# Half filter convolution: branch bodies of 48 products in place of 80, and one branch for each added stage in place of one for three

## The chip, the cores and the metric

The kernel runs on one core of a Trainium2 chip. The metric is the time of one execution on the device in microseconds (us), the median of the runs. Five engines work side by side: TensorE (PE in the profile; PEld is its weight load), VectorE (DVE), ScalarE (ACT), GpSimd (POOL) and SyncE (SP), which starts the loads.

## The reference, cut to what matters

The model is a convolution block, a mixture of experts, attention, and the mixture again. The change lies in the convolution:

```
n_blocks, block_size, ks = (128, 64, 16)
n_block_row = n_channels // block_size          # n_channels = 256 here: 4
cols = randint(k3, (n_blocks,), 0, n_block_row)
rows = randint(k4, (n_blocks,), 0, n_block_row)
...
o = conv1d(x_unfold, W, padding=[(ks - 1, 0)], feature_group_count=n_blocks)
y = zeros(batch, n_block_row, bs, t).at[:, rows].add(o)
```

Each of 128 blocks of 64 by 64 by 16 weights filters one group of 64 input channels (`cols`) and is added to one group of 64 output channels (`rows`). The input has 512 channels, so 8 groups exist, but the drawn `cols` and `rows` are 0 to 3. The kernel must be right for 0 to 7 too.

## The kernel before

The weights of all blocks with the same pair of input and output group are summed first, and the convolution is then done with the sums. The 16 taps are handled as 8 stages `st` of two taps each.

Stages 0 to 4 (`NPE = 5`): TensorE sums. A stage has 8 banks; `sum_bank(st, q)` (line 647) waits for 512 KB of weights and multiplies them, in 8 products of 64 columns (16 matmuls on the chip), by a one-hot matrix. `raw` is a ring of 6 loads, so the bank numbered c+6 is loaded when bank c is summed. ScalarE rounds each bank (`round_banks`), VectorE takes the low part (`low_banks`, line 505), and `sum_bank` of bank c waits for the low part of bank c-3.

Stages 5 to 7 (`ND = 3`, the added stages): VectorE adds each of the 128 blocks into `acc` (`add_block`, line 524, the groups named `cv_acc` at line 532), and these additions are spread between the `low_banks` of stages 1 to 4: 14 blocks ahead of stage 2, then 4, 5 and some 5 for each bank. Their weights come in 16 loads of 768 KB from GpSimd's queue (`tap_blocks`), in a ring of three.

`products` (line 657, matmuls at line 669) is the convolution proper: three matmuls of 256 columns for each of four input groups `c` and two row groups `r`, for the pairs of the lower half (0 to 3). The products of stages 0 to 4 are woven between the banks of the next stage. After the last product of a stage comes `finish_products(st)`: a wait, a branch, and a matmul with zeros (line 696) that gives ScalarE the slot free. Where any block has a row or column of 4 or more, `flag` is 1, and the branch body runs `high_products(st)`, the pairs outside the lower half. With the drawn inputs `flag` is 0 and the body is skipped; line 689 has no instruction in the profile.

`convolve_added` ends the phase: it waits for the low part of the first added piece, passes one branch whose body has `high_products` of all three added stages, closes the banks of the two upper row groups (`close`, line 700), which lets VectorE add them to `X`, and runs ten pieces of 12 matmuls in the order of `LAST_PRODUCTS`, each behind its own wait. Ahead of the last piece it transposes the first half of the next phase's input (line 133). The next phase's first matmul is at line 1255.

`high_products` of one stage loops over 8 input groups and 4 row groups without the lower quarter: 8 cases with six products each and 16 cases with two products each, all fp32 with 256 columns.

Of the kernel before, what the change touches and what calls it, by code (L numbers as in the profile page):

```python
# [11 lines left out]
F32 = mybir.dt.float32  # L12
# [7 lines left out]
P = 128  # L20

B, C, D = 2, 512, 256
# [5 lines left out]
NCB = C // BS  # L28
NST = KS // 2
XPITCH = 272  # L30
M = D // 2
# [3 lines left out]
NPE, ND = 5, 3  # L35
# [130 lines left out]
def conv_phase(nc, cm, pm, ps, ins, following, prefetch, first_weights):  # L166


    with ExitStack() as ctx:
# [7 lines left out]
        X0, XA, XB, X1 = range(4)  # L177
# [3 lines left out]
        xc_hi, xc_lo = (sb(f"xc_{part}", [P, NCB // 2, B, 3, SPITCH], F32R) for part in ("hi", "lo"))  # L181
        xp = sb("xp", [P, NCB // 2, B, XPITCH], F32)
# [56 lines left out]
        def pair_index(c, row):  # L239

            return c * (NCB // 2) + row + (c >= NCB // 2) * (NW // 4) + (row >= NCB // 2) * (NLOW - NCB // 2)
# [4 lines left out]
        def piece_of(f, r):  # L246
            return NPE * SB + ADDED_ORDER.index((f, r))
# [382 lines left out]
        def tensor(t):  # L630
# [26 lines left out]
            def products(f, c, r):  # L657

                w = pair_index(c, 2 * r)
                if f >= FIR:  # L660
                    stream, tap, bank = X0, 2 * (f - FIR), ps[P2_BANK][:, r * D:(r + 1) * D]
                else:
                    h = 1 - f % 2
                    stream, tap, bank = (XA, XB)[h], 2 * (f // 2), ps[4 + r][:, h * D:(h + 1) * D]
                hi, lo = (x[:, c, :, stream, tap:tap + M] for x in (xc_hi, xc_lo))
                w_hi, w_lo = (x[SLOT[f]][:, w:w + 2, :].rearrange("p c o -> p (c o)") for x in (ws_hi, ws_lo))
                last = c == NCB // 2 - 1 and (f, r) in LAST_OF
                for n, (lhs, rhs) in enumerate(((w_hi, hi), (w_lo, hi), (w_hi, lo))):
                    m = t.matmul(bank, lhs, rhs, start=False, stop=last and n == 2)  # L669
                if last:  # L670
                    m.then_inc(s["conv_done"], 1)

            def high_products(st):

                tap = 2 * (st // 2)
                for c in range(NCB):
                    for r in range(GC):
                        if c < NCB // 2 and r < GC // 2:
                            continue
                        w, h = pair_index(c, 2 * r), 1 - st % 2  # L680
                        sums = (full[st % 2][:, w:w + 2, :] if st < NPE else acc[:, st - NPE, w:w + 2, :]).rearrange("p c o -> p (c o)")
                        if c >= NCB // 2:
                            base = 2 * tap + h
                            moving = [(p, xp[:, c - NCB // 2, :, base + p:base + p + 2 * M - 1:2]) for p in range(2)]
                        else:
                            moving = [(p, x[:, c, :, stream, tap:tap + M].bitcast(F32)) for x in (xc_hi, xc_lo)
                                      for p, stream in ((0, X0), (1, X0), (h, (XA, XB)[h]))]
                        for p, x in moving:
                            t.matmul(ps[4 + r][:, p * D:(p + 1) * D], sums, x, start=False, stop=False)

            def finish_products(st):
                t.wait_ge(s["ws_lo_done"], (st + 1) * SB)
                with t.If(flag != 0):
                    t.wait_ge(s["ws_lo_done"], (st + 1) * SB)
                    high_products(st)
                t.matmul(ps[4][:, 0:1], zeros[:, 0:P], zeros[:, 0:1], start=False, stop=False)\
                 .then_inc(s["ws_free"], 1)

            def close(r):
                t.matmul(ps[4 + r][:, 0:1], zeros[:, 0:P], zeros[:, 0:1], start=False, stop=True)\  # L700
                 .then_inc(s["conv_done"], 1)

            def convolve_added():
                for n, (f, r) in enumerate(LAST_PRODUCTS):
                    t.wait_ge(s["ws_lo_done"], piece_of(f, r) + 1)
                    if n == 0:
                        with t.If(flag != 0):
                            t.wait_ge(s["added"], 2 + 2 * NBLK)
                            for st in range(NPE, NST):
                                high_products(st)  # L710
                        for upper in (2, 3):
                            close(upper)
                    if n == len(LAST_PRODUCTS) - 1:
                        following["turn"](t)
                    for c in range(NCB // 2):
                        products(f, c, r)
# [39 lines left out]
            for u in units(4):  # L756
                products(*u)
            finish_products(4)
            convolve_added()

    def ended(e):
# [1395 lines left out]
```

## Time and profile before

| | |
|---|---|
| median of 3 runs | 912.01 us (911.85 to 912.79) |
| the profiled execution | 915.21 us |
| span from its first to its last instruction | 913.4 us |
| PE busy | 892.1 us, 98% |
| granted TensorE clock, mean | 0.955 |

Times in the views are microseconds from the first instruction; the convolution takes the first 165 of them. A busy PE is not a fast PE: the granted clock is shown apart, 1.00 for 2.4 GHz and 0.50 for 1.2 GHz. An idle time marked "issue" is one in which the engine waited for nothing that the view shows. The queue "q8 instruction" carries program code.

### The profile page before, as it was taken

Reading aid. Unit: us, or ns where it says so; the run is one execution under the profiler, and the core shown is the slowest. Engines: PE = TensorE matmul, PEld = TensorE weight load, DVE = VectorE, ACT = ScalarE, POOL = GpSimd, SP = SyncE. Lnnn points to the kernel's source line nnn. Section 1 sums busy time; section 2 is a strip of 40 time slices with the busy share of each in tenths; the row PEclk is TensorE's granted clock in tenths of the full one; section 3 lists DMA queues with packets and bytes.
Section 4 is the critical chain, followed back from the end, with each engine's and each line's share of the span. In section 5 each row is a group of like instructions: output and inputs, shape, how many; then the busy total and the mean of one; then the engine's idle time right before and its main releaser. Section 6 shows DMA issues by size and latency. Waiting matters only on the chain.

```text
span 913.4 us, 16920 instructions
## 1 busy us (share of the span) xinstructions
PE 892.1 (98%) x5680; PEld 806.7 (88%) x5680; DVE 518.8 (57%) x1366; ACT 427.7 (47%) x984; POOL 351.6 (38%) x330
## 2 busy tenths in 40 slices
PE   9999896999999999999999999999999999999998
PEld 7899896788888888888998998999898888888887
DVE  4764657653333333788768867876877633333334
ACT  4522213543343343577647647765764534343342
POOL 6811203245655565412212121221202455655562
PEclk9956767999999999999999999999999999999999
DMA  8986720211111111200100010000001111111111
GB/s 339 329 280 224 289 79 4 87 52 52 35 51 52 52 34 36 72 1 24 36 1 23 0 34 0 23 0 1 1 1 52 36 53 52 38 48 52 52 34 47
DMA packets 25559, 61.09 MB, mean 67 GB/s; under 512 B 3298, under 2 KB 10916, under 8 KB 25508
## 3 DMA queue, kind: packets, MB, share of 16 engines
q1 hardware_dynamic: 23204, 47.82, 15.7%
q0 software_dynamic: 2304, 12.58, 3.9%
q8 instruction: 32, 0.52, 0.3%
q14 instruction: 19, 0.16, 0.1%
HBM read 59.35 MB, written 1.05 MB: 66 GB/s over the span
## 4 chain that ended last, share of the span: by engine, by line
PE 89%; DVE 5%; ACT 2%; issue 2%; POOL 2%; DVEq 0%; ACTq 0%; POOLq 0%
PE bank L1255 27%; PE bank L1779 22%; PE bank L1268 14%; PE bank L653 8%; PE bank L669 4%; PE bank L1905 4%; PE bank L1845 2%; PE bank L1281 2%; PE bank L1291 2%; ACT at_prob L1474 1%; POOL cv_xp L386 1%; PE bank L1870 1%; PE bank L637 1%; DVE at_smax L1662 1%; DVE cv_late L516 0%
## 5 line engine op out<-in xcount | busy, mean ns | idle before, releaser
L1154 DVE TENSOR_TENSOR f_h<-f_scaled,bank 128x512 f32<-128x512 f32 (+1 forms) x90 | 60.9, 676 | 179.4 <-POOL f_scaled L1019 166.9
L936 ACT ACTIVATE f_h_hi<-f_h 128x512 fp32r<-128x512 f32 (+2 forms) x102 | 63.6, 624 | 185.5 <-DVE f_h L1154 185.3
L1019 POOL TENSOR_TENSOR f_scaled<-f_act,f_gate_rows 128x512 f32<-128x512 f32 x80 | 103.0, 1288 | 116.1 <-ACT f_act L929 115.8
L1255 PE MATMUL bank<-f_xt_hi,f_w_lo 128*128 128x512 f32 x352 | 138.2, 393 | 0.0
L1255 PE MATMUL bank<-f_xt_hi,f_w_hi 128*128 128x512 f32 x352 | 137.8, 391 | 0.0
L1161 DVE TENSOR_TENSOR f_h_lo<-f_h,f_h_hi 128x512 fp32r<-128x512 f32 (+2 forms) x102 | 71.8, 704 | 70.7 <-ACT f_h_hi L936 70.2
L1474 ACT ACTIVATE at_prob<-bank,at_sbias,at_qrs 128x512 f32<-128x512 f32 (+3 forms) x128 | 77.8, 618 | 72.4 <-DVE at_sbias L1666 72.3
L1255 PE MATMUL bank<-f_xt_lo,f_w_hi 128*128 128x512 f32 x352 | 108.8, 390 | 0.0
L1268 PE MATMUL bank<-f_w_lo,f_h_hi 128*128 128x256 f32 (+1 forms) x352 | 99.6, 283 | 0.0
L1268 PE MATMUL bank<-f_w_hi,f_h_lo 128*128 128x256 f32 (+1 forms) x352 | 99.6, 283 | 0.0
L1268 PE MATMUL bank<-f_w_hi,f_h_hi 128*128 128x256 f32 (+1 forms) x352 | 99.3, 282 | 0.0
L1537 POOL TENSOR_TENSOR at_qrs<-at_qsum,minus_half 128x4 f32<-128x4 f32 x32 | 32.9, 1027 | 137.8 <-DVE at_qsum L1627 137.8
L929 ACT ACTIVATE f_act<-bank 128x512 f32<-128x512 f32 (+2 forms) x102 | 59.9, 589 | 52.5 <-PE bank L1255 46.3
L1255 PEld LDWEIGHTS bank<-f_xt_lo,f_w_hi 128*128 128x128 f32 x352 | 66.1, 188 | 14.4
L1255 PEld LDWEIGHTS bank<-f_xt_hi,f_w_lo 128*128 128x128 f32 x352 | 66.4, 189 | 11.1
L1255 PEld LDWEIGHTS bank<-f_xt_hi,f_w_hi 128*128 128x128 f32 x352 | 66.5, 189 | 11.0
L1268 PEld LDWEIGHTS bank<-f_w_hi,f_h_lo 128*128 128x128 f32 (+1 forms) x352 | 67.2, 191 | 3.4
L1268 PEld LDWEIGHTS bank<-f_w_hi,f_h_hi 128*128 128x128 f32 (+1 forms) x352 | 67.2, 191 | 3.3
L1008 POOL TENSOR_TENSOR f_w_lo<-f_wraw,f_w_hi 128x512 fp32r<-128x512 f32 x46 | 59.5, 1295 | 25.3 <-ACT f_w_hi L915 25.3
L309 ACT ACTIVATE cv_full<-bank 128x512 f32<-128x512 f32 x40 | 23.9, 598 | 93.2 <-PE bank L653 92.7
L1268 PEld LDWEIGHTS bank<-f_w_lo,f_h_hi 128*128 128x128 f32 (+1 forms) x352 | 67.2, 191 | 0.0
L653 PE MATMUL bank<-cv_onehot,cv_raw 128*128 128x64 f32 x416 | 65.0, 330 | 1.9 <-issue 1.7
(252 smaller groups left out, 2216.8 us busy)
## 6 DMA issues: line engine op xcount, KB each, us to landing
cv_raw<-in_wconv SPq DMA_DIRECT2D x26, 512.0 KB, 5.5
cv_shared<-in_wtaps POOLq DMA_DIRECT2D x16, 768.0 KB, 6.0
f_wraw<-in_w SPq DMA_DIRECT2D x42, 256.0 KB, 2.6
xn<-in_wconv SPq DMA_DIRECT2D x14, 512.0 KB, 5.5
f_wraw<-in_w SPq DMA_DIRECT2D x42, 128.0 KB, 2.5
at_wraw<-in_wqkv SPq DMA_DIRECT2D x3, 768.0 KB, 4.4
at_oraw<-in_wo SPq DMA_DIRECT2D x4, 512.0 KB, 3.5
X<-in_x_tiles SPq DMA_DIRECT2D x2, 512.0 KB, 8.3
```

Source lines behind the costliest of these rows:

```text
L653: m = t.matmul(ps[c % BANKS][:].rearrange("p (w o) -> p w o", o=OB)[:, :, o], raw[c % RING][:, o * P:(o + 1) * P], onehot[:], start=True, ...
L669: m = t.matmul(bank, lhs, rhs, start=False, stop=last and n == 2)
L929: a.activation(act[half][0:rows, cols], pg[half][0:rows, cols], ACT.Silu).then_inc(s["act_done"], 1)
L936: a.activation(h_hi[slot][0:rows, cols], h_f[half][0:rows, cols], ACT.Copy).then_inc(s["h_hi_done"], 1)
L1008: g.tensor_tensor(w_lo[slot][:, 0:n], raw_views(m, slot, rows)[0], w_hi[slot][:, 0:n].bitcast(F32), ALU.subtract).then_inc(s["w13_lo_done" ...
L1019: g.tensor_tensor(scaled[half][:], act[half][:], gate_rows[:, half * HALF:(half + 1) * HALF], ALU.mult).then_inc(s["scaled_done"], 1)
L1154: v.tensor_tensor(h_f[half][0:rows, cols], src[half][0:rows, cols], pu[half][0:rows, cols], ALU.mult)\
L1161: v.tensor_tensor(h_lo[slot][0:rows, cols], h_f[half][0:rows, cols], h_hi[slot][0:rows, cols].bitcast(F32), ALU.subtract).then_inc(s["h_lo ...
L1255: mm = t.matmul((pg, pu)[gu][half][0:out_rows, :], w, x, start=q == 0, stop=q == 3 * KH - 1)
L1268: mm = t.matmul(bank, h[hslot][0:rows, tok], w, start=first and q == 0 and j % 2 == 0, stop=False, skip_group_check=True)
L1474: a.activation(prob[:, sl, POFF[j]:POFF[j + 1]], ps[bank][:, col:col + n], ACT.Exp, bias=sbias[:, sl, j:j + 1], scale=qrs[:, sl, j:j + 1], ...
L1779: m = t.matmul(dst, l, r, start=start and q == 0, stop=stop and q == 2, skip_group_check=in_opened_bank)
```

## The change

Three things. The two phases of an input row are taken by one product of 512 columns in place of two of 256: the 16 cases with two products have one, and of the other 8 each set of three becomes one product of 512 and one of 256. Products of `high_products` fall from 80 to 48. In `convolve_added` the one branch with the three added stages becomes three branches, ahead of the pieces 0, 1 and 2, each with one stage. And the two `close` matmuls move from ahead of piece 0 to ahead of piece 2.

```
@@ high_products
-  moving = [(p, xp[:, c - NCB // 2, :, base + p:base + p + 2 * M - 1:2]) for p in range(2)]
-  else:
-      moving = [(p, x[:, c, :, stream, tap:tap + M].bitcast(F32)) for x in (xc_hi, xc_lo)
-                for p, stream in ((0, X0), (1, X0), (h, (XA, XB)[h]))]
-  for p, x in moving:
-      t.matmul(ps[4 + r][:, p * D:(p + 1) * D], sums, x, start=False, stop=False)
+  row = xp[:, c - NCB // 2, :, base:base + D].rearrange("p b (m h) -> p h b m", h=2)
+  t.matmul(ps[4 + r][:], sums, row, start=False, stop=False)
+  continue
+  for x in (xc_hi, xc_lo):
+      common, part = (x[:, c, :, stream, tap:tap + M].bitcast(F32) for stream in (X0, (XA, XB)[h]))
+      t.matmul(ps[4 + r][:], sums, common.unsqueeze(1).to_broadcast([P, 2, B, M]), start=False, stop=False)
+      t.matmul(ps[4 + r][:, h * D:(h + 1) * D], sums, part, start=False, stop=False)
@@ convolve_added
   t.wait_ge(s["ws_lo_done"], piece_of(f, r) + 1)
-  if n == 0:
+  if n < ND:
       with t.If(flag != 0):
           t.wait_ge(s["added"], 2 + 2 * NBLK)
-          for st in range(NPE, NST):
-              high_products(st)
+          high_products(NPE + n)
+  if n == ND - 1:
       for upper in (2, 3):
           close(upper)
```

## Rows read from the trace of the kernel before

**Rows 1.** The page: granted clock in 40 slices, and the queue of code.
```profile
PEclk9956767999999999999999999999999999999999
...
q8 instruction: 32, 0.52, 0.3%
```

**Rows 2.** Stretches: length, busy time of each engine, granted clock, DMA share, GB/s.
```profile
7.30:36.30 29.00, 28.85 (x256) 28.67 (x256) 21.36 (x55) 18.14 (x38) 24.10 (x21) 1.00 0.97 363
...
39.80:43.20 3.40, 1.67 (x17) 1.64 (x15) 2.35 (x10) 0.00 (x0) 1.94 (x4) 1.00 0.93 280
43.20:84.20 41.00, 41.00 (x194) 40.91 (x193) 21.18 (x103) 8.72 (x21) 6.08 (x8) 0.50 0.73 257
84.20:97.90 13.70, 13.70 (x123) 13.70 (x121) 10.16 (x53) 4.32 (x11) 4.53 (x8) 1.00 0.78 271
97.90:101.20 3.30, 0.26 (x3) 0.05 (x1) 2.84 (x16) 0.27 (x2) 1.13 (x2) 1.00 1.00 396
101.20:132.00 30.80, 30.21 (x142) 30.22 (x143) 17.72 (x87) 6.30 (x15) 4.08 (x4) 0.50 0.46 171
...
138.80:142.20 3.40, 0.68 (x6) 0.40 (x4) 3.40 (x4) 2.35 (x5) 3.40 (x3) 1.00 0.06 10
142.20:149.00 6.80, 1.64 (x8) 1.55 (x9) 6.80 (x9) 3.76 (x7) 2.76 (x2) 0.50 0.01 2
...
152.40:165.30 12.90, 12.90 (x109) 12.90 (x108) 6.14 (x16) 1.09 (x2) 1.21 (x2) 1.00 0.00 0
```

**Rows 3.** Timeline of PE at the six skips: start, length, line, count, idle before.
```profile
42.44 1.95 PE L653 MATMUL bank<-cv_onehot,cv_raw 128*128 128x64 f32 x12 [1.73 <-issue]
...
72.25 0.23 PE L696 MATMUL bank<-zeros 128*128 128x1 bf16 x1
...
101.79 0.19 PE L696 MATMUL bank<-zeros 128*128 128x1 bf16 x1 [3.63 <-issue]
...
140.67 0.18 PE L696 MATMUL bank<-zeros 128*128 128x1 bf16 x1 [1.36 <-issue]
145.51 0.21 PE L700 MATMUL bank<-zeros 128*128 128x1 bf16 x2 [4.67 <-DVE cv_late L516]
...
148.85 0.37 PE L669 MATMUL bank<-cv_xc_lo,held 128*128 128x256 f32 x1 [1.86 <-issue]
```

**Rows 4.** PE groups by shape, 0 to 165.3 us: count, busy, mean ns.
```profile
L653 PE MATMUL bank<-cv_onehot,cv_raw 128*128 128x64 f32 x416 | 65.0, 330 | 1.9 <-issue 1.7
```

**Rows 5.** DMA, code packets in 16-17, 29-30, 40-41, 99-101, 136-149.5 us.
```profile
q8 instruction: 1, 0.02, 6.7%
...
q8 instruction: 1, 0.02, 6.8%
...
q8 instruction: 1, 0.02, 6.3%
...
q8 instruction: 1, 0.02, 3.1%
...
q8 instruction: 4, 0.07, 2.7%
```

**Rows 6.** Timeline of DVE: the waits and low parts that pace PE.
```profile
45.02 2.11 DVE L532 TENSOR_TENSOR cv_acc<-cv_acc,cv_shared 128x96 f32 x12 [2.88 <-DMA cv_shared<-in_wtaps]
...
52.82 0.28 DVE L509 TENSOR_TENSOR held<-bank,held 128x128 fp32r<-128x128 f32 x1
...
137.67 1.23 DVE L516 TENSOR_TENSOR held<-cv_acc,held 128x512 fp32r<-128x512 f32 x1 [0.78 <-ACT held L321]
...
148.33 0.68 DVE L463 TENSOR_TENSOR X<-X,bank 128x512 f32<-128x512 f32 x1
```

**Rows 7.** The stretch 53 to 126 us, columns as in rows 2.
```profile
53.00:126.00 73.00, 69.37 (x382) 69.07 (x382) 40.05 (x201) 15.49 (x39) 12.90 (x20) 0.62 0.67 239
```

**Rows 8.** Timeline of PE: two banks at half clock, and the phase's end.
```profile
59.45 6.92 PE L653 MATMUL bank<-cv_onehot,cv_raw 128*128 128x64 f32 x32
...
165.25 0.39 PE L1255 MATMUL bank<-f_xt_hi,first_hi 128*112 128x512 f32 x1
```

## The prediction

> **What bounds the kernel now.** I read the page first: PE is busy 98% and is the bound throughout, but its granted clock dips in the slices of the convolution and nowhere else [rows 1]. Nothing of the change executes: `flag` is 0 and the bodies are skipped, so no saved matmul can save time. What is left is how far PE's code has to jump, and when.
>
> Next I looked at PE around the six skips [rows 3]. Skips 1 to 5 jump over the same body (320 instructions, below) and cost very differently: 1.73 us of idle time among the thin matmuls behind the first, none at the second (72.25), 3.63 us at the third, again none at the fourth (136.2), 1.36 us at the fifth. The sixth jumps three times as far: 4.67 us, and 1.86 us more five matmuls later. The view calls five of these gaps "issue"; it puts the 4.67 down to VectorE, but the one piece that the skip waits for was done at 137.67 + 1.23 = 138.90 [rows 6], before PE even came to it at 140.85. The gaps have packets of code inside or just ahead of them: one at 40 to 41 us, one at 99 to 101, and four in the 13.5 us around the last three gaps [rows 5]. So PE waited for code. Code comes in packets of 0.52 MB / 32 = 16 KB [rows 1].
>
> Last, the granted clock [rows 2]. PE worked at 2.4 GHz from 7.3 to 36.3, on nothing but the thin 64-column matmuls. It fell to 1.2 GHz at 43.2, 101.2 and 142.2, each time right behind a stretch with a code gap: PE was busy 1.67 of 3.40, 0.26 of 3.30 and 0.68 of 3.40 us. Then it stayed low for 41.0, 30.8 and 10.2 us although PE was fully busy for most of that, and rose each time behind dense 256-column products. A bank of 16 thin matmuls takes 28.85 / 16 = 1.80 us at 2.4 GHz [rows 2] and 6.92 / 2 = 3.46 us at 1.2 GHz [rows 8]; a product matmul 12.90 / 109 = 0.118 us, say 0.120 [rows 2], and 256 columns at 1.2 GHz are 0.213 us. The gaps are 13.3 us in sum; the low clock behind them costs more.
>
> **The change part by part.** *Distance.* The 8 fp32 products of each of 40 banks, 320 in all, stand as 640 matmuls (416 in this group [rows 4], 224 in the one of the other two buffers), each with its own weight load, so a product is 4 instructions. A body falls from 80 x 4 = 320 to 48 x 4 = 192, the sixth from 960 to three of 192. How many instructions are in a packet? From the one at 16 to 17 to the one at 29 to 30 us [rows 5] PE went on for some 13.3 us, 119 thin matmuls with their loads and 8 waits: about 250. A jump of 320 leaves its packet always and crosses two borders if it starts in the last third; one of 192 crosses one at most. If the next packet is asked for on entering the present one, a jump of 192 always lands on code that is there or due, while 320 sometimes lands beyond. That fits skips 1 to 5: two jumped too far (the third and fifth), one landed just short of a border and ran into it (the first). I expect the first three costs to go: 1.73, 3.63 and 1.36 us to about 0. Bounds: 0 and all 6.7.
>
> *The clock behind the gaps.* Without the gap PE is busy through 39.8 to 43.2 on thin matmuls, as in the first stretch, which held 2.4 GHz [rows 2]. But at full speed PE runs into VectorE: its additions wait for a load until 45.02, and bank 21 needs the low part of bank 18, done at 52.82 + 0.28 = 53.10 [rows 6]. So bank 21 starts at 53.1, not 59.45 [rows 8]. From there three resources work side by side. PE needs 19 banks x 1.80 + 138 product matmuls x 0.120 = 50.8 us. DMA has 73.0 x 0.67 = 48.9 us of transfers left, VectorE 40.1 us [rows 7]. With PE at full clock the DMA share was 0.97 (7.3 to 36.3) and 0.78 (84.2 to 97.9) [rows 2]; I take 0.90: 54.3 us, to 107.4, and about 4 us for the last additions and products, 111. Before, this point is 140.67 - 1.36 = 139.3 [rows 3]. That is 28 us less if the clock holds.
>
> It may not. [...] One more fall costs about 1.6 us for each bank as far as PE was the bound; in the last stage the loads allow a bank each 3 us, so that 8 banks at 3.46 and 48 products at 0.093 more are some 6 us. Bounds: 0, and for a clock that stays low from 50 us to the dense products at the end: 17 banks x 3.46 + 84 x 0.213 from 53.1 gives 129.8, plus 7 for the rest, 137: only 2 us won.
>
> *The tail.* A missing packet takes 148.85 - 145.51 = 3.34 us from entry to use, with DMA otherwise quiet [rows 3]. Three jumps of 192 with 24 instructions (a piece of 12 matmuls, 1.44 us) between them cross about 2.5 packets, so each next one is waited for: the first comes about 1.9 us behind the last product of stage 4 (its packet was asked for at the fifth skip), then 3.34 and 3.34 with the pieces 0 and 1 inside. Piece 2 starts 8.6 us behind 139.2, at 147.8 on the old scale, with 96 product matmuls (11.5 us) and eight transposes (0.9) to go: 160.2 in place of 165.25 [rows 8]. PE is busy 1.44 of each 3.34 us in 256-column products, four times as wide as the thin ones, so I let the clock hold; if it falls the 5.0 shrink to about 1. I take 4.5.
>
> *The moved closes.* VectorE adds the upper rows at 148.33, behind its ten low parts and not behind the closes at 145.5 [rows 3, 6]; closes at 147.8 are still ahead of it. If PE comes later, each us delays these sums, their statistics and then `add_common`, which waits for piece 4 anyway. Cost 0, bound 1. The two added branches and the 2 instructions they add are under 0.2 us (skip 2 shows no gap). The code behind moves by 1022 instructions, four packets less two; loops lie as before: 0.
>
> The Trainium skill (TensorE: Matmul & The Clock Gate, "What's actually happening") has an idle engine throttled and released soon after sustained work resumes. The trace disagrees on the release: 41 us low at full occupancy [rows 2]. By that rule the low stretches would be short and only the gaps would count.
>
> **The rivals.**
> A, the clock holds to the tail: 28 + 4.5, so 912.0 - 32.5 = 879.5. For it: 29 us of thin work at 2.4 GHz. Against it: PE will be starved.
> B, it falls once more, at the start of the last stage or near 50 us, and recovers at dense products: 28 - 5.5 + 4.5 = 27, 885.0.
> C, it falls near 50 us and stays low to the end of the last stage: 2 + 4.5, 905.5. For it: 41 us low in rows 2. By the page's rule above the result would be near here too, from the other side: 13.3 us of gaps less about 5.7 left in the tail, 904.
> D, the change doesn't do what it says: waiting for code hangs on how often one jumps, not how far. Against it: two skips without a gap. 912.
> E, slower: every jump pays a full fetch, since a packet asked for on entry comes late beside the loads. The third skip's packet came at 99 to 101, over 3 us behind the jump. Eight skips x 3.63 = 29.0 against 13.3, +15.7 with the clock low as before: 927.7. It decides if jumps are closer than a fetch; those of the stages are over 13 us apart, only the tail's are not.
>
> **How the numbers follow.** A 0.32, B 0.43, C 0.14, D 0.04, E 0.07. The sum is made against the profiled 915.21 us (span 913.4), 3.2 above the median; the difference is put on the median 912.01. The likeliest is B, 885.0, its own range 879 to 893 (DMA share 0.97 to 0.80 is -4 to +7). The range reaches from A with a better share, 876, to the near side of C, 904; beyond it lie the rest of C, D and E, some 0.2. 0.2% (1.8 us) is what can be told from no change. Faster 0.90, same 0.04, slower 0.06.
>
> **What would show it.** After: no "issue" gap at line 653 near 40 us and none over 0.5 us at line 696; granted clock 1.00 from 43 to at least 50 us; DMA share 0.85 or more between 50 and 105; three gaps of about 2 us before line 669's last pieces, in place of 4.67 and 1.86; the first matmul of line 1255 between 132 and 142 us. The prediction is wrong if the clock falls at 43 all the same, if a gap reappears in another stage because the packet's border lies elsewhere, or if VectorE's waits for `cv_shared` grow as the two load queues meet.

## The result, and the profile after

The changed kernel takes 890.8 us (median of 4, 889.5 to 892.97) beside 912.4 us (4 runs) for the kernel before on the same chip: a ratio of 0.9764, 95% interval 0.9741 to 0.9788, or 21.6 us. The forecast was 27 us less, 885.0, in a range of 876 to 904. The profiled execution took 891.64 us, its span 889.8 us, and its mean granted clock is 0.977 in place of 0.955. Medians and ratios in this document leave out an execution more than 1.5% above the fastest of the same kernel; there is one each of e4, e10 and e12 (1067.55, 916.16 and 951.61 us). In the changed kernel the lines behind `high_products` are one higher: 696 is now 697, 700 is 701 and 1255 is 1256. In the experiments they move again with each edit; it is the same matmul with zeros behind each skip, and the same closes.

The page of the changed kernel shows the clock in 40 slices and the queue of code, as in [rows 1]:

```profile
PEclk9978789999999999999999999999999999999999
...
q8 instruction: 29, 0.48, 0.2%
```

Three fewer packets of code are fetched. The dip of the clock is shallower and shorter, but it is still there. The timeline of PE has these rows at the places of [rows 3] and [rows 8] (start, length, line, count, idle time before):

```profile
39.79 3.77 PE L653 MATMUL bank<-cv_onehot,cv_raw 128*128 128x64 f32 x32
...
52.42 1.75 PE L653 MATMUL bank<-cv_onehot,cv_raw 128*128 128x64 f32 x14 [1.12 <-DVE held L509]
...
98.14 2.09 PE L653 MATMUL bank<-cv_onehot,xn 128*128 128x64 f32 x13 [0.91 <-DVE held L509]
...
119.72 0.18 PE L697 MATMUL bank<-zeros 128*128 128x1 bf16 x1
...
121.63 0.50 PE L669 MATMUL bank<-cv_xc_hi,held 128*128 128x256 f32 x2 [1.73 <-issue]
...
125.14 0.79 PE L669 MATMUL bank<-cv_xc_hi,cv_late 128*128 128x256 f32 x2 [1.70 <-issue]
...
128.24 0.21 PE L701 MATMUL bank<-zeros 128*128 128x1 bf16 x2 [0.17 <-issue]
...
141.69 0.39 PE L1256 MATMUL bank<-f_xt_hi,first_hi 128*112 128x512 f32 x1
```

The 1.73 us behind the first skip are gone: 32 thin matmuls run on from 39.79. So are the 3.63 and the 1.36. Stage 4's last product ends at 119.9 us (119.72 + 0.18) where it was 139.3, 19.4 us earlier. From there to the next phase's first matmul it now takes 141.69 - 119.9 = 21.8 us, and it was 165.25 - 139.3 = 25.95: 4.15 us less. Together 23.6 us lie in the convolution. That is the 913.4 - 889.8 of the two spans, so nothing moved in the rest of the kernel; the medians differ by 21.6.

The chain of waits for PE up to 150 us (in total, times, longest) names what is left:

```profile
PE bank L669 <- issue: 3.4, 2, 1.7
PE bank L653 <- DVE held L509: 2.6, 3, 1.1
...
PE bank L701 <- issue: 0.2, 1, 0.2
```

The windows, with columns as in [rows 2], show where the clock went:

```profile
39.80:43.20 3.40, 3.40 (x33) 3.40 (x32) 2.62 (x10) 0.77 (x2) 2.12 (x5) 1.00 0.87 284
43.20:52.40 9.20, 7.55 (x64) 7.13 (x63) 7.80 (x31) 4.06 (x9) 3.00 (x3) 1.00 0.98 388
52.40:54.80 2.40, 2.38 (x21) 2.37 (x21) 2.27 (x14) 0.38 (x1) 0.58 (x1) 1.00 1.00 404
54.80:75.30 20.50, 20.50 (x98) 20.41 (x98) 10.74 (x59) 3.45 (x10) 2.56 (x5) 0.50 0.80 293
75.30:99.20 23.90, 22.99 (x204) 22.84 (x202) 17.66 (x91) 8.60 (x21) 6.10 (x11) 1.00 0.90 322
99.20:112.80 13.60, 13.60 (x66) 13.60 (x65) 12.63 (x59) 2.30 (x6) 3.49 (x3) 0.50 0.52 186
...
119.90:123.10 3.20, 1.47 (x12) 1.47 (x12) 3.20 (x3) 2.13 (x5) 3.20 (x3) 0.99 0.02 5
123.10:129.90 6.80, 4.92 (x23) 4.32 (x23) 6.76 (x9) 3.47 (x6) 2.46 (x2) 0.50 0.02 5
...
50.00:105.00 55.00, 52.98 (x356) 52.52 (x355) 38.52 (x188) 13.96 (x35) 12.94 (x20) 0.76 0.86 316
```

The clock does not fall at 43. It holds for 11.6 us longer, until PE has run up against VectorE: three waits for a low part (0.55 us at 46.66, 1.12 at 52.42, 0.91 at 98.14). Behind the second it falls for 20.5 us, behind the third for 13.6, and behind the first code gap of the tail for 6.8. That makes 40.9 us at 1.2 GHz in place of 41.0 + 30.8 + 10.2 = 82.0 [rows 2].

Who is behind those waits for VectorE? Its own timeline:

```profile
44.20 2.11 DVE L532 TENSOR_TENSOR cv_acc<-cv_acc,cv_shared 128x96 f32 x12 [1.78 <-DMA cv_shared<-in_wtaps]
...
48.35 3.73 DVE L532 TENSOR_TENSOR cv_acc<-cv_acc,cv_shared 128x96 f32 x8
52.00 0.28 DVE L509 TENSOR_TENSOR held<-bank,held 128x128 fp32r<-128x128 f32 x1
...
128.34 0.68 DVE L516 TENSOR_TENSOR cv_ws_lo<-cv_acc,cv_ws_hi 128x512 fp32r<-128x512 f32 x1
128.94 0.68 DVE L463 TENSOR_TENSOR X<-X,bank 128x512 f32<-128x512 f32 x1
```

Twelve additions wait 1.78 us for a load, and a little later eight take 3.73 us where twelve took 2.11: one of the eight lasts 2.55 us where the median is 0.25, which I read as a second such wait. The kernel before has a group like it, eight in 3.75 us at 49.15. The load is late, the additions wait for it, the low part stands behind the additions in VectorE's order, and PE is named as waiting for VectorE. The last row answers to [rows 6]: the sum of the upper rows still stands directly behind the last low part, so the moved closes cost nothing.

### The profile page after: what moved, and what is told of

Same layout as the page of the kernel before. It is cut to its first block, busy times and chain, and to the rows that moved or that the text cites. A ratio compares the mean times of both kernels' runs of the same rounds, so it can differ in the third digit from the quotient of the medians.

```text
span 889.8 us, 16919 instructions
## 1 busy us (share of the span) xinstructions
PE 875.5 (98%) x5677; PEld 789.4 (89%) x5680; DVE 518.2 (58%) x1366; ACT 427.5 (48%) x984; POOL 351.3 (39%) x330
## 4 chain that ended last, share of the span: by engine, by line
PE 87%; DVE 6%; issue 2%; POOL 2%; DMA 2%; ACT 1%; DVEq 0%; ACTq 0%; POOLq 0%
PE bank L1256 28%; PE bank L1780 24%; PE bank L1269 14%; PE bank L653 4%; PE bank L669 4%; PE bank L1906 4%; PE bank L1846 2%; PE bank L1282 2%; PE bank L1292 2%; DMA cv_shared<-in_wtaps 2%; DVE cv_acc L532 1%; POOL cv_xp L386 1%; PE bank L1871 1%; PE bank L637 1%; ACT at_prob L1475 1%
## 5 line engine op out<-in xcount | busy, mean ns | idle before, releaser
L532 DVE TENSOR_TENSOR cv_acc<-cv_acc,cv_shared 128x96 f32 x256 | 54.6, 283 | 10.1 <-issue 5.1
L1663 DVE TENSOR_REDUCE at_smax<-bank 128x1 f32<-128x512 f32 (+3 forms) x128 | 58.6, 485 | 2.3 <-PE bank L1780 2.0
```

Source lines behind the costliest of these rows:

```text
L532: add = v.tensor_tensor(dst, dst, src, ALU.add)
L1663: v.tensor_reduce(smax[:, sl, j:j + 1], ps[bank][:, col:col + P * (j + 1)], AX_X, ALU.max)\
```

## The experiments

Each kernel is the one before or the changed one with the edit shown. The ratio is to the kernel before on the same chip, whose median there is 913.17 us for e1 to e4, 912.12 for e5 to e8 and 914.1 for e9 to e12; runs of different groups are best compared by it. "Clock" is the mean granted clock of the profiled execution; "stages end" is the end of stage 4's last product, "next phase" its first matmul, both in us of that execution.

| kernel | median us | ratio to before (95%) | clock | stages end | next phase |
|---|---|---|---|---|---|
| before | 912.4 | 1 | 0.955 | 139.3 | 165.25 |
| after | 890.8 | 0.9764 (0.9741 to 0.9788) | 0.977 | 119.9 | 141.69 |
| e1_one_branch | 893.27 | 0.9775 (0.9731 to 0.982) | 0.975 | 121.5 | 144.32 |
| e2_long_bodies | 914.56 | 1.0014 (0.9998 to 1.003) | 0.957 | 137.7 | 165.04 |
| e4_padded | 908.5 | 0.9944 (0.9923 to 0.9964) | 0.957 | 139.9 | 161.64 |
| e3_no_branch | 891.19 | 0.976 (0.972 to 0.98) | 0.981 | 122.8 | 141.11 |
| e5_moved | 902.11 | 0.9878 (0.9856 to 0.99) | 0.966 | 132.5 | 154.26 |
| e7_spaced | 883.14 | 0.9661 (0.9614 to 0.9708) | 0.978 | 121.1 | 140.16 |
| e6_dense_zeros | 879.39 | 0.9635 (0.9614 to 0.9657) | 0.998 | 107.8 | 129.94 |
| e8_dense_at_skips | 906.96 | 0.9925 (0.9897 to 0.9952) | 0.957 | 139.2 | 164.72 |
| e10_dense_in_gaps | 904.73 | 0.9879 (0.9853 to 0.9906) | 0.975 | 129.0 | 155.13 |
| e11_dense_no_branch | 879.38 | 0.9628 (0.9594 to 0.9662) | 0.998 | 108.9 | 128.24 |
| e12_dense_long | 904.56 | 0.9899 (0.988 to 0.9919) | 0.977 | 125.6 | 152.91 |
| e9_dense_spaced | 878.65 | 0.9615 (0.9599 to 0.9631) | 1.000 | 108.0 | 127.88 |

### Which part of the change does it: e1, e2

e1 keeps the short bodies and puts the three stages back behind one branch, with the closes ahead of piece 0. e2 keeps the bodies of 80 and splits the branch, with the closes moved.

```
e1, from the changed kernel
-  if n < ND:
+  if n == 0:
       with t.If(flag != 0):
           t.wait_ge(s["added"], 2 + 2 * NBLK)
-          high_products(NPE + n)
-  if n == ND - 1:
+          for st in range(NPE, NST):
+              high_products(st)
       for upper in (2, 3):
           close(upper)
```

e2 is the same edit the other way round, from the kernel before.

> The kernel after the change, with the one branch for the three added stages kept (its body is 576 instructions in place of 960) and both closes ahead of piece 0, as before. Theory 1 (a skip costs by where it lands in the 16 KB packets of code): the stages 0 to 4 go as in the changed kernel; the skip of 576 lands two packets on, 15 instructions ahead of a border, so PE waits once for about 3.5 to 4.7 us and once more for about 1.9 us, as at the sixth skip before; the three waits of the changed kernel (1.73, 1.70 and under 0.6 us) go. About 893 us, 1 to 4 us over the changed kernel. Rival (each added branch costs a fetch): fewer branches, so 2 to 5 us under the changed kernel, 887.

> The kernel before, with its bodies of 80 products, and only the three branches of the change in place of the one. Theory 1: the code of stages 0 to 4 lies exactly as before, so the gaps of 1.73, 3.63 and 1.36 us and the low clock from 43 to 84 and from 101 to 132 us stay; only the tail changes, by -3 to +3 us: 909 to 915 us. Rival (the three branches and the moved closes bring the gain): about 891 us.

e1 gives 893.27 and e2 914.56, both inside what my theory expected. The shorter bodies alone bring all but about 2 us, and the intervals of e1 and after overlap; the split branch and the moved closes alone bring nothing (ratio 1.0014, interval 0.9998 to 1.003).

### Is it the length of what is jumped over: e4

The changed kernel with its bodies in stages 0 to 4 filled up to the old length, with products that never run:

```
   with t.If(flag != 0):
       ...
       high_products(st)
+      for _ in range(64):
+          t.matmul(ps[4][:, 0:1], zeros[:, 0:P], zeros[:, 0:1], start=False, stop=False)
```

> The changed kernel, with 64 small products with zeros (128 instructions) behind the 48 products in the bodies of stages 0 to 4, so that these bodies are 320 instructions long again; nothing of them runs. Theory 1: distance alone counts, so the gaps of about 1.7 us near 40 us, 3.6 us near 98 us and 1.4 us near 140 us come back, and with them 1.2 GHz from 43 to 84 and from 101 to 132 us: 909 to 914 us. Rival (the wider products or fewer of them matter in themselves): stays at 891 us.

908.5 us, just under the 909 to 914 that I expected: code that isn't executed takes back all but 4.7 us (3.3 to 7.0 by the interval). The timeline of PE shows that it brings the gaps back one for one with [rows 3]:

```profile
42.83 4.14 PE L653 MATMUL bank<-cv_onehot,cv_raw 128*128 128x64 f32 x23 [2.00 <-issue]
...
102.46 0.19 PE L699 MATMUL bank<-zeros 128*128 128x1 bf16 x1 [3.96 <-issue]
...
141.52 0.18 PE L699 MATMUL bank<-zeros 128*128 128x1 bf16 x1 [1.61 <-issue]
```

Stage 4 ends at 139.9 us again, and the next phase starts 21.7 us later, as in the changed kernel. So the tail's gain of 4.15 us doesn't hang on the stages' gain, and it is about what e4 keeps.

### Is it the length, or the place where the jump lands: e5

From the kernel before, only the body of stage 0 is made longer, by 64 matmuls (128 instructions), so that every later jump starts half a packet further on.

```
   high_products(st)
+  for _ in range(64 if st == 0 else 0):
+      t.matmul(ps[4][:, 0:1], zeros[:, 0:P], zeros[:, 0:1], start=False, stop=False)
```

> The kernel before, with 64 small products with zeros (128 instructions) more in the body of stage 0 alone, which is never run; all later code lies half a packet further on. Theory 1: the first skip (448) now jumps over a whole packet and waits at its landing, 3.5 to 6 us in place of 1.73, and the clock falls at 43 us as before; the second skip still finds its packet but runs into a border 27 instructions behind it, which may cost up to 2 us at 1.2 GHz; the third skip now lands on the next packet, so the gap of 3.63 us near 98 us is gone and the clock stays at 2.4 GHz there until VectorE or a load is waited for; the fourth skip misses (up to 3 us, near 136 us), the fifth doesn't. Sum: +2 to +4 for the first, -3.6 and about -10 for the third, +1 to +2 for the fourth less 1.4 for the fifth: 898 to 906 us. Rival (a longer body costs more, wherever it lies): 912 us or more, the third gap still 3.6 us.

902.11 us: a longer body that never runs makes the kernel 1.2% faster. Positions counted in the compiled code, with 256 instructions to a packet of 16 KB (skip, packet of the branch, packet of its target, instructions from there to the next border, idle time of PE):

```
        before                        e5_moved
skip 1   2 ->  3   22   1.73 us        2 ->  4  150   2.82 us
skip 2   5 ->  6  155   none           5 ->  6   27   none
skip 3   7 ->  9  240   3.63           8 ->  9  112   none
skip 4  10 -> 11   69   none          10 -> 12  197   1.33
skip 5  11 -> 13  210   1.36          12 -> 13   82   none
skip 6  13 -> 16   15   4.67 + 1.86   13 -> 17  143   4.63
```

Every jump over two borders or more stalls, in both kernels. The records of the branches themselves, which the views leave out, say the same: skips 3, 5 and 6 last 5.84, 3.56 and 4.73 us in the kernel before, the other three 0.34 to 0.41; in e5 skips 1, 4 and 6 last 5.03, 3.67 and 4.73 us. Skip 5 of e5 crosses one border and still lasts 2.32 us, without idle time of PE; it starts 50 instructions behind the landing of skip 4. A landing 22 or 15 instructions short of a border stalls too, unless PE is slow enough to be covered (skip 2 of e5, 27 short, at 1.2 GHz). The rows of e5 for skips 1, 4, 5 and 6:

```profile
41.72 0.18 PE L698 MATMUL bank<-zeros 128*128 128x1 bf16 x1 [2.82 <-issue]
...
129.09 0.18 PE L698 MATMUL bank<-zeros 128*128 128x1 bf16 x1 [1.33 <-issue]
...
132.33 0.18 PE L698 MATMUL bank<-zeros 128*128 128x1 bf16 x1
137.14 0.20 PE L702 MATMUL bank<-zeros 128*128 128x1 bf16 x2 [4.63 <-DVE cv_late L516]
```

Skip 3 cost 3.63 us and a fall of 30.8 us before; without it the clock is low there for only 13.6 us (110.0 to 123.6). The first fall, with a gap of 2.82 us ahead of it, is still 44.4 us long (41.7 to 86.1). The 4.63 us under VectorE's name belong to skip 6, as the 4.67 did: the branch lasts 4.73 us in both.

The Trainium skill (Runtime: NRT & Kernel Launch, "Instruction fetch mechanics") says that a taken branch whose target lies outside the two pages at hand forces a fetch. The jumps over two borders agree: PE stood idle behind them for 3.63 and 1.36 us here, and for 2.82 and 1.33 in e5. Landings 22 and 15 instructions short of a border cost 1.73 and 1.86 us as well.

### What would be left without any jump: e3

The changed kernel without its branches and bodies; the pairs outside the lower half are left out.

> All branches around the products of the upper pairs left out, and those products with them (they never run with these inputs). Theory 1: no gap at line 653, 669, 697 or 701 that is marked issue; PE and the clock in the stages as in the changed kernel, because there the clock falls at waits for VectorE and the loads, not for code; the tail loses its 3.6 us of gaps and its 6.8 us at 1.2 GHz: about 884 us, between 881 and 888. Rival (the low clock in the changed kernel still comes from code): no fall at all, 875 us or less.

I missed here: I expected 884 us, and it is 891.19, the same as the changed kernel. PE's timeline, and two windows:

```profile
47.70 1.97 PE L653 MATMUL bank<-cv_onehot,xn 128*128 128x64 f32 x16 [1.74 <-DVE held L509]
...
52.78 2.58 PE L653 MATMUL bank<-cv_onehot,cv_raw 128*128 128x64 f32 x11 [3.11 <-DVE held L509]
```

```profile
43.20:50.60 7.40, 4.73 (x40) 4.42 (x39) 4.67 (x18) 3.29 (x7) 1.69 (x2) 1.00 0.96 384
50.60:77.90 27.30, 25.12 (x118) 25.06 (x118) 15.37 (x78) 3.83 (x10) 3.89 (x6) 0.50 0.71 244
```

There is no gap of code left in it, and the clock still falls, for 27.3 and 6.9 us. So the falls that the changed kernel keeps in its stages have another cause than code: PE, now fast, waits for VectorE and the loads behind it. The tail does get shorter, 141.11 - 122.8 = 18.3 us against 21.8, but in this execution the stages end 2.9 us later: the waits for VectorE were longer (6.8 us in sum, where the changed kernel has 2.6), and the first fall came earlier. My expectation had counted the tail and taken the stages as fixed.

### The tail alone: e7

The changed kernel with its added branches ahead of pieces 0, 2 and 4 in place of 0, 1 and 2, the closes at 4.

```
-  if n < ND:
+  if n in (0, 2, 4):
       ...
-          high_products(NPE + n)
-  if n == ND - 1:
+          high_products(NPE + n // 2)
+  if n == 4:
```

> The changed kernel, with the three added branches ahead of the pieces 0, 2 and 4 in place of 0, 1 and 2, and the closes ahead of piece 4. Theory 1: two pieces (2.9 us at 2.4 GHz) lie between two skips, nearly the 3.3 us that a packet takes, so the gaps shrink to about 1.7 us, 0.5 and 0.5 and the clock doesn't fall at 123 us; the closes are about as late as they are now: 2 to 5 us under the changed kernel, 886 to 889 us. Rival (VectorE's sums of the upper rows set the end of the phase, and later closes delay them): same or up to 2 us slower.

883.14 us. Only one code gap is left, 1.82 us at 121.1. The direction is as expected, the size isn't settled: the four runs lie at 890.69, 886.97, 879.31 and 879.05, and the one with a profile is the slowest of them. It shows a tail of 140.16 - 121.1 = 19.1 us, 2.7 us less than after, and still a fall in it, of some 3 us. The faster ones have no trace, but their mean granted clock is on record: 0.978, 0.982, 0.992 and 0.995, in the same order. Half of the time at 1.2 GHz is missing from the mean, so that the first had some 39 us of it and the last some 9. That is more than the tail's falls, so falls in the stages stayed away too, and no run shows that the spaced branches are the cause of that. What the spacing is worth by itself is the 2.7 us of the tail.

### Holding the clock: e6, and e9 with e7's branches

Two products with zeros, 512 columns wide, ahead of each bank of stages 2 and 4. They add nothing to the sums, and add work to PE.

```
   c = st * SB + q
+  for _ in range(2 if st in (2, 4) else 0):
+      t.matmul(ps[4][:], zeros[:, 0:P], zeros[:], start=False, stop=False)
```

> The changed kernel, with two products of 512 columns with zeros ahead of each bank of stages 2 and 4 (0.43 us at 2.4 GHz for each bank, 6.8 us of PE work in all, added onto an open accumulator, so nothing is changed). Theory 1 (the clock falls where PE is starved of wide work for some us): the falls at 54.8 and 99.2 us don't come, or one of them; PE then keeps 2.4 GHz, paced by loads and VectorE: stages 2 to 4 end 5 to 10 us earlier, 881 to 887 us. Rival (the clock's falls cost little, since the loads set the pace anyway): the added work shows, 890 to 897 us.

> The changed kernel with both edits of the last two runs: two products of 512 columns with zeros ahead of each bank of stages 2 and 4, and the three added branches ahead of the pieces 0, 2 and 4 with the closes ahead of piece 4. Theory 1: the clock stays at 2.4 GHz to the end of stage 4 (879.4 us with that alone), and the tail has two of its three code gaps smaller: 1 to 4 us under 879.4, 875 to 878 us. Rival (with the clock held, VectorE's ten low parts set the tail, so its gaps are free): 878 to 881 us.

e6 gives 879.39 us, below what I expected, 881 to 887; 11.4 us less than after by adding work. Its windows:

```profile
43.20:104.00 60.80, 60.06 (x502) 57.36 (x507) 51.30 (x251) 19.61 (x48) 17.04 (x23) 1.00 0.89 344
...
116.20:119.60 3.40, 3.40 (x18) 3.40 (x18) 3.37 (x7) 0.00 (x0) 0.00 (x0) 0.50 0.02 5
```

The clock holds through all stages. They end at 107.8 us, 31.5 us ahead of the kernel before. In e9 it never falls:

```profile
43.20:104.00 60.80, 60.15 (x504) 57.02 (x504) 50.08 (x250) 19.61 (x48) 15.78 (x22) 1.00 0.89 342
104.00:114.00 10.00, 7.39 (x59) 6.80 (x57) 9.22 (x20) 5.52 (x10) 6.34 (x4) 1.00 0.01 3
```

and this is the lowest median, 878.65 us, with the closest runs, 878.47 to 878.9; by the ratios it can't be told from e6 (0.9615 and 0.9635, the intervals overlap). I had expected 875 to 878 for it, and the rival 878 to 881. The number alone doesn't part the two, since the kernel before is 2.0 us slower on this chip than on e6's. The timeline speaks for the rival, in which VectorE then sets the tail. It has no code gap there, but these:

```profile
109.05 0.50 PE L671 MATMUL bank<-cv_xc_hi,held 128*128 128x256 f32 x2 [1.01 <-DVE held L516]
111.97 0.51 PE L671 MATMUL bank<-cv_xc_hi,cv_late 128*128 128x256 f32 x2 [1.24 <-DVE cv_late L516]
114.71 0.51 PE L671 MATMUL bank<-cv_xc_hi,cv_late 128*128 128x256 f32 x2 [1.07 <-DVE cv_late L516]
```

The three branches last 0.40 to 0.41 us each, so that none of these waits is one for code. In e6 the third branch of the tail lasts 1.53 us.

### With the clock held, what do the jumps cost: e11, e12

e11 is e6 without branches and bodies; the pairs outside the lower half are left out. e12 puts e6's zero products into the kernel before, and shortens two bodies that don't run by as many instructions, so that the jumps land where they did; skips 2 and 4 start 32 instructions later.

> All branches and their bodies left out (the products for upper pairs, which never run here), with two products of 512 columns with zeros ahead of each bank of stages 2 and 4. No code gap and, by theory 1, no fall of the clock before the tail. Against 879.4 us for the changed kernel with the same zeros it shows what the code gaps that are left (1.68 and 1.74 us in the tail) cost once the clock holds: theory 1, 2 to 4 us, 875 to 878 us. Rival (VectorE's low parts set the tail): 878 to 881 us.

> The kernel before, bodies of 320 instructions, with two products of 512 columns with zeros ahead of each bank of stages 2 and 4 (the bodies of stages 1 and 3 are 8 products shorter, so that the code of the skips lies as before). The skips keep their gaps of 1.7, 3.6 and 1.4 us and the tail its 4.7 and 1.9. Theory 1: against the same zeros in the changed kernel (879.4 us) it shows what the gaps cost where the clock is mostly held: the five gaps less those of the changed kernel are 9.9 us, and some falls come back at 43 or 101 us: 888 to 898 us. Rival (the low clock before doesn't hang on how wide PE's work is): 912 us or more, the added 6.8 us on top.

e11 gives 879.38 and e6 879.39: once the clock holds, the jumps of the changed kernel cost nothing that can be measured (0.9628 and 0.9635, each to within some 3 us). The profiled executions show more. Without branches the tail is 128.24 - 108.9 = 19.3 us long where e6 has 22.1, so the jumps do cost there; but e11 lost some 2 us again behind it, where its clock fell for about 3 us at 133, in the next phase.

e12 gives 904.56, more than I expected (888 to 898). With e6 and the two kernels of the case it makes a square. By the ratios, long jumps cost 2.4% without the zeros and 2.6% with them; the zeros bring 1.3% with short jumps and 1.0% with long ones. The intervals are 0.2% on each side of a ratio, so the square doesn't show that either change hangs on the other. The zeros shorten the falls, they don't prevent those that a code gap starts. The first is now 13.7 us long, where it was 41.0, and the second 17.1 us, where it was 30.8:

```profile
42.00:55.70 13.70, 13.60 (x60) 12.41 (x59) 9.27 (x39) 3.35 (x7) 3.91 (x4) 0.50 0.80 289
```

### Gap or clock, which is the dearer: e8, e10

In the kernel before, zero products are put only ahead of skips 1 and 3, again with bodies shortened so that the code stays in place: 4 and 4 in e8, 8 and 16 in e10. The edit of e10:

```
+  dense = {0: 8, 2: 16}.get(st, 0)
+  for _ in range(dense):
+      t.matmul(ps[4][:], zeros[:, 0:P], zeros[:], start=False, stop=False)
   with t.If(flag != 0):
       ...
-      high_products(st)
+      high_products(st, dense // 2)
```

The second argument leaves out that many products of the body.

> The kernel before, with four products of 512 columns with zeros ahead of the first and of the third skip, and two products less in each of those two bodies (which never run), so that all code lies as before. The gaps of code stay: about 0.9 us (1.73 less 0.85 of new work) near 41 us and about 3 to 4 us near 98 us. Theory 1 (what the gap costs is the clock that it lets fall): with the wide work in the same stretch the clock doesn't fall at 43 us, and runs at 2.4 GHz until VectorE is waited for, near 52 us: 5 to 15 us under the kernel before, 897 to 907 us. Rival (the clock falls at 43 us for another reason, or the gap itself is the cost): no gain, 911 to 914 us.

> The kernel before, with 8 and 16 products of 512 columns with zeros ahead of the first and third skip (1.7 and 3.4 us of PE work, about as long as the gaps of code behind these skips) and as many instructions less in the two bodies, which never run: all code lies as before, and PE goes on past each skip as late as before, but busy. Theory 1: the time lost at the skips stays and the clock doesn't fall at 43 and 101 us; it falls only where VectorE is waited for, as in the changed kernel: 893 to 901 us, 11 to 19 us under the kernel before. Rival (the time lies in the gaps themselves): 912 us.

e8 is inconclusive. Its median, 906.96, lies within the expected 897 to 907, but the execution with a profile took 914.62, and in it the gap (2.19 us) and the fall at 43 are both there; the faster ones, 903.51 to 907.87, have no trace. Their mean granted clock is 0.968 to 0.973, against 0.957 in the profiled one, so they spent less time at 1.2 GHz; where, isn't known. e10 gives 904.73, short of the expected 893 to 901. Its timeline has no gap at skip 1: the thin matmuls go on right behind the zero products. The clock no longer falls at 43, so PE comes to skip 2 at full speed, and there a gap opens where the kernel before had none:

```profile
63.51 0.19 PE L703 MATMUL bank<-zeros 128*128 128x1 bf16 x1 [2.75 <-issue]
...
92.75 0.18 PE L703 MATMUL bank<-zeros 128*128 128x1 bf16 x1 [2.34 <-issue]
```

Skip 2 stands 36 instructions behind a border, so its target's packet has just been asked for. I read it so that at half clock these instructions covered the fetch, and at full clock they don't. The branch lasts 4.93 us here and 0.41 in the kernel before. In e12 PE comes to skip 2 at full clock too, and there is no gap: the branch stands 32 instructions further behind the border, and zero products stand ahead of it. Behind the gap at skip 2 the clock is 0.50 from 64 to 70 us, and behind the 2.34 us at skip 3 the clock fell for 27.3 us all the same:

```profile
94.10:121.40 27.30, 27.30 (x130) 27.30 (x130) 16.36 (x79) 6.30 (x15) 4.07 (x4) 0.50 0.40 139
```

So e10 shows that time spent at skip 1 costs little if it is spent on dense products, and that the fall behind it is the larger part: PE is past skip 2 at 63.51 us where it was 72.25, 8.7 us earlier, although 1.7 us of zero products and the gap of 2.75 us have come in. It does not give a clean price of one fall.

## Why the prediction was right, and where its size was off

**The distance.** Right. All three gaps of the stages went to 0 as stated, with none over 0.5 us before line 697. e4 (the distance alone brings them back) and e5 (each jump over two borders stalls, and a jump over one doesn't, unless it lands close to a border or starts soon after its packet was entered) show the mechanism. Rival D falls, and so does E: eight skips, three gaps, 3.6 us in all. One premise of E was misread: not all jumps of the stages are over 13 us apart. The fourth and the fifth are 4.5 us apart in the kernel before (136.2 and 140.67) and 3.0 in the changed one (116.76 and 119.72), and there neither of them has a gap. Rows 3 alone had been enough to tell which of the six skips crossed two borders; the count in the code confirms each.

**The clock behind the gaps.** Right in kind: it didn't fall at 43 and held to 54.8. The prediction's point that PE would then wait for VectorE's low part of bank 18, and bank 21 start at 53.1, is the row at 52.42. The DMA share between 50 and 105 is 0.86, the sign asked for 0.85.

**The term that was mis-sized** is "one more fall, 5.5 us". There were two in the stages, of 20.5 and 13.6 us. With the clock held, stages 0 to 4 end at 107.8 us (e6), 31.5 us earlier and not 28, so that the 28 was 3.5 us too small; measured from there the two falls cost 119.9 - 107.8 = 12.1 us, not 5.5. The working of the one fall didn't add up either: 8 banks at 3.46 us where the loads allow one each 3 us are 3.7 us, 48 products at 0.093 are 4.5, and that is 8.2, not "some 6". Together the stages gave 19.4 us, not 22.5. Rival C, low from 50 to the end of the stages, was too dark: the clock came back twice, at 75.3 and 112.8. The stretch between them, from 75.3 to 99.2, ran at 1.00 beside a DMA share of 0.90, just the share that I had taken.

**Why it falls again.** The three long waits, the fall behind each of the last two, and e3, which has no jump and falls all the same, point to PE waiting for VectorE, and show that no code is needed for it. The load of `cv_shared` behind VectorE is read from one timeline; no run took that load away. One of the prediction's own signs of being wrong did come: VectorE's waits for `cv_shared` between 30 and 130 us grew, from 3.3 us in two waits to 4.4 us in four. The gain was there all the same.

**The tail.** Right in size by two errors. I expected three gaps of 1.9 us with the clock held, and 4.5 us less. The gaps were 1.73, 1.70 and 0.17 us, and the clock fell at 123.1: the third gap is small because the twelve products ahead of it took twice as long and covered the fetch (the third branch itself lasts 2.94 us, 125.24 to 128.18). Four packets of code come in between 119 and 130 us:

```profile
q8 instruction: 4, 0.07, 2.4%
```

The gain is 4.15 us. Under e9, with no gap of code and no fall, the tail still takes 127.88 - 108.0 = 19.9 us, since VectorE's low parts are then late.

**The moved closes and the added branches** cost nothing that the medians of e1 and e2 show (e2: 1.0014, at most 1.003). In the profiled execution of e2 the tail is 165.04 - 137.7 = 27.3 us, 1.4 us longer than before, within the 3 us that e2 was given.

**The forecast.** B, 885.0, was 5.8 us too low, because of the falls in the stages. A's time, 879.5, is what e6 takes (879.39), but that is partly luck: the stages gave 31.5 us there, not 28, and the tail 25.95 - 22.1 = 3.8, not 4.5, and the 35.4 us between the two profiled spans are 33.0 between the medians.

## What to carry to other kernels

Code that never runs has a price: its length and its place decide whether a taken branch lands on code that is there, so count the instructions of a skipped body against the size of a packet, keep it under one, and keep the branches apart. Price a short idle time of TensorE by the stretch at 1.2 GHz that follows it, not by itself: here three waits of 2.6 us in sum stood ahead of 34.1 us of low clock. Where TensorE is paced by loads with narrow matmuls and waits, wide products with zeros put ahead of the waits can make the kernel faster: they took off 1.3% here with the long jumps gone, and 1.0% with them still there.

## What the runs showed that I had not expected

- A longer body that isn't executed made the kernel faster: +128 instructions, 912.12 to 902.11 us (e5). The prediction had no word of it; e5's own forecast, 898 to 906, did.
- Adding 32 wide products with zeros took 11.4 us off (e6), more than the 4 to 10 that e6 had been expected to gain; without the shorter bodies the same products took off 9.5 us beside the kernel before on the same chip (e12).
- Removing every branch brought nothing to the median (891.19 against 890.8), with the clock free to fall (e3) or held (879.38 against 879.39, e11).
- The clock fell in stretches with only short waits, 1.12 us ahead of the fall at 54.8, and then stayed at 1.2 GHz for 20.5 us with PE busy for 20.50 of them.
- A skip that cost nothing at 1.2 GHz cost 2.75 us at 2.4 GHz (skip 2 of e10): cover has to be counted at the clock at which it will run.
